# Block-quantizer scale computed straight from the block maximum, and layernorm statistics of the next tile taken before the transposes of this one

## What is computed

```python
def fp4_quant_dequant(x):                    # blocks of 16 along the last dim
    scale = jnp.max(jnp.abs(xb), axis=-1, keepdims=True) / 6.0
    scale = jnp.maximum(scale, jnp.float32(1e-12))
    xn = xb / scale
    idx = jnp.searchsorted(_MID, jnp.abs(xn))
    q = _GRID[idx] * jnp.sign(xn) * scale

mod = (_silu(c) @ wmod).reshape(B, 6, 1, -1)   # sa, ca, ga, sb, cb, gb
h = _layernorm(x) * (1 + ca) + sa
x = x + ga * attention(h, wq, wk, wv, wo)      # causal softmax, rope
h = _layernorm(x) * (1 + cb) + sb
gate, y = fp4_linear(h, w_gate), fp4_linear(h, w_up)
x = x + gb * fp4_linear(silu(gate) * y, w_down)
```

## Time and profile before

| what | value |
|---|---|
| time, median of 2 runs | 11339.54 us (11335.91 to 11343.18) |
| the profiled execution, its own time | 11276.26 us |
| its span, slowest core (core 4) | 11274.7 us |
| spans of the 8 cores | 11165.9 to 11274.7 us |
| VectorE busy on core 4 | 6960.9 us (62%) |
| TensorE matmul busy on core 4 | 5694.6 us (51%) |
| ScalarE busy on core 4 | 1098.6 us (10%) |

### The profile page before, as it was taken

One profiled execution on the slowest core, in us unless ns is written; L12 is line 12 of the kernel. 1 busy time (PEld: TensorE's weight loads), 2 busy tenths in 40 slices (PEclk: granted clock), 3 DMA queues, 4 the chain that ended last, 5 costly groups with the idle time before them and its releaser, 6 DMA issues.

```text
span 11274.7 us, 79773 instructions; the slowest of 8 cores (11165.9 to 11274.7 us)
## 1 busy us (share of the span) xinstructions
PE 5694.6 (51%) x20690; PEld 2189.5 (19%) x21080; DVE 6960.9 (62%) x17486; ACT 1098.6 (10%) x2066; POOL 100.6 (1%) x120
## 2 busy tenths in 40 slices
PE   1000156766675577467845454444554444544455
PEld 0000022212221222122212222222222222212222
DVE  6787753335324532443257777777777777777777
ACT  0000000220122013102300000000000000000000
POOL 0000000000000000000000000000000000000000
PEclk5555567766676788687867677767776777777777
DMA  3101121011101200211020000000000000000000
GB/s 66 49 30 55 50 32 30 30 36 25 30 30 43 25 23 30 52 15 38 15 82 15 12 12 13 14 12 12 15 10 14 12 14 13 10 14 12 15 12 12
DMA packets 181185, 289.77 MB, mean 26 GB/s; under 512 B 106428, under 2 KB 118972, under 8 KB 179720
## 3 DMA queue, kind: packets, MB, share of 16 engines
q1 hardware_dynamic: 63688, 237.28, 6.1%
q0 software_dynamic: 117056, 47.36, 3.6%
HBM read 247.45 MB, written 84.51 MB: 29 GB/s over the span
## 4 chain that ended last, share of the span: by engine, by line
DVE 43%; PE 28%; DVEq 13%; issue 7%; DMA 6%; ACT 2%; another core or an unknown queue 1%; POOL 1%; SPq 0%; ACTq 0%; POOLq 0%
DVEq L91 12%; PE pG L959 3%; PE pG L753 3%; PE pG L628 2%; DMA xt<-xmid_scr 2%; PE pA L607 2%; PE pA L705 2%; PE pB L607 2%; PE pEF L735 2%; PE pG L735 2%; DVE qd_g_f L443 2%; PE pC L730 2%; PE pH L939 2%; DVE qd_q_f L443 2%; PE pD L730 2%
## 5 line engine op out<-in xcount | busy, mean ns | idle before, releaser
L886 PE MATMUL pA<-wgT,xqf 128*128 128x512 bf16 x1461 | 633.7, 434 | 1157.7 <-DVE hmid L918 983.6
L959 PE MATMUL pG<-wdT,hqf 128*128 128x512 bf16 x2740 | 1006.7, 542 | 193.8 <-DVE hqf L944 186.5
L939 PE MATMUL pH<-identb,hq_t 128*128 128x128 bf16 x1408 | 180.6, 306 | 1288.5 <-DVEq L926 1288.5
L675 DVE COPY recipb<-pG 128x512 f32<-128x512 f32 x128 | 88.5, 692 | 1057.2 <-PE pG L669 1057.2
L892 PE MATMUL pC<-wuT,xqf 128*128 128x512 bf16 x1536 | 663.0, 432 | 44.2 <-DVE xqf L866 39.7
L726 ACT ACTIVATE union<-pA 128x512 bf16<-128x512 f32 (+1 forms) x640 | 354.7, 554 | 2759.3 <-PE pA L711 1717.3
L892 PE MATMUL pD<-wuT,xqf 128*128 128x512 bf16 (+1 forms) x1536 | 592.3, 386 | 6.0 <-issue 3.5
L886 PE MATMUL pB<-wgT,xqf 128*128 128x512 bf16 (+1 forms) x1473 | 570.3, 387 | 0.0
L959 PEld LDWEIGHTS pG<-wdT,hqf 128*128 128x128 bf16 x2816 | 352.5, 130 | 798.6 <-issue 732.2
L607 PE MATMUL pA<-union,wbuf 128*128 128x512 bf16 x1004 | 320.4, 473 | 260.7 <-DVE stag L613 103.0
L753 PE MATMUL pG<-union 128*128 128x512 bf16 x1000 | 340.9, 512 | 203.5 <-DVE xw L768 166.8
(11 more groups left out here) (163 smaller groups left out, 10556.1 us busy)
## 6 DMA issues: line engine op xcount, KB each, us to landing
xt<-x SPq DMA_DIRECT2D x128, 512.0 KB, 4.1
xmid_scr<-xw SPq DMA_DIRECT2D x64, 512.0 KB, 2.9
xt<-xmid_scr SPq DMA_DIRECT2D x64, 512.0 KB, 4.2
out<-xw SPq DMA_DIRECT2D x64, 512.0 KB, 2.8
wmb<-wmod POOLq DMA_DIRECT2D x12, 1024.0 KB, 10.4
wbuf<-wq POOLq DMA_DIRECT2D x32, 256.0 KB, 7.6
wbuf<-wk POOLq DMA_DIRECT2D x32, 256.0 KB, 6.9
wbuf<-wv POOLq DMA_DIRECT2D x32, 256.0 KB, 7.2
```

The source lines that it names most:

```text
L886: self.op('T', lambda E, cc=c, o=io, w=iw, p=pGt: E.matmul(p[:, 0:w], self.xqf[:, cc, :], self.wgT[:, cc, o:o + w], start=(cc == 0), stop= ...
L939: self.op('T', lambda E, cc=c, k2=kk, hq=hqt[i]: E.transpose(pH[:, k2, :], hq[:, cc * 128:(cc + 1) * 128], self.identb[:]), chT if kk == n ...
L959: st=(ib == 0 and c == 0), sp=lastd: E.matmul(pG[:, ha * 512:(ha + 1) * 512], self.hqf[:, k2, :], self.wdT[:, ig, ha * 512:(ha + 1) * 512] ...
```

## The change

Two edits that don't depend on each other.

In `_emit_qd` the intermediate `sc` is gone. The reciprocal is taken of `bm` itself, `scb` is computed from `bm` as `max(bm/6, 1e-12)`, and the factor 12 goes into the first constant of L423's instruction. One `tensor_scalar` for each piece and one fence for each call are removed. `scb`'s instruction now has two operations on its way (multiply, maximum), as the removed one had.

In stage A1 the load, the wait for it and the statistics of tile tc+1 are put between the layernorm of tile tc and the transposes and copy of tile tc. `_emit_ln_mod` is split into its two halves for this. TensorE's wait for `chV` stays the statement after them.

```diff
@@ _emit_qd
         each(lambda srcp, dstp, pw, nbl, src3, rs_b, sc_b, s:
-             V('V', lambda E: E.tensor_scalar(s['sc'][:, 0:nbl], s['bm'][:, 0:nbl],
-                                              1.0 / 12.0, 5e-13, ALU.mult, ALU.max)))
-        dr('V')
+             V('V', lambda E: E.reciprocal(s['rs'][:, 0:nbl], s['bm'][:, 0:nbl])))
         each(lambda srcp, dstp, pw, nbl, src3, rs_b, sc_b, s:
-             V('V', lambda E: E.reciprocal(s['rs'][:, 0:nbl], s['sc'][:, 0:nbl])))
-        each(lambda srcp, dstp, pw, nbl, src3, rs_b, sc_b, s:
-             V('V', lambda E: E.tensor_scalar(s['scb'][:, 0:nbl], s['sc'][:, 0:nbl],
-                                              2.0, None, ALU.mult)))
+             V('V', lambda E: E.tensor_scalar(s['scb'][:, 0:nbl], s['bm'][:, 0:nbl],
+                                              1.0 / 6.0, 1e-12, ALU.mult, ALU.max)))
         dr('V')
         each(lambda srcp, dstp, pw, nbl, src3, rs_b, sc_b, s:
              V('V', lambda E: E.scalar_tensor_tensor(
-                 s['xn'][:, 0:pw].rearrange("p (a b) -> p a b", b=16), src3, 1.0,
+                 s['xn'][:, 0:pw].rearrange("p (a b) -> p a b", b=16), src3, 12.0,
                  rs_b, ALU.mult, ALU.mult)))
@@ _emit_attention, stage A1
-        for tc in range(NTC):
+        def a1_stats(tc):
             b = tc % 2
             self.waitm('Y', self.r_xt.guard())
             self.dma('Y', self.xt[b][:], self.x_in[s, tc * 128:(tc + 1) * 128, :], dX[b])
             self.wait('V', dX[b])
-            self._emit_ln_mod(self.xt[b][:], self.hmod_t[:])
+            return self._emit_ln_stats(self.xt[b][:])
+
+        smark = a1_stats(0)
+        for tc in range(NTC):
+            b = tc % 2
+            self._emit_ln_apply(self.xt[b][:], self.hmod_t[:], smark)
             self.r_xt.done(chV)
+            if tc + 1 < NTC:
+                smark = a1_stats(tc + 1)
             self.wait('T', chV)
             self.waitm('T', self.r_pH.guard())
             for c in range(8):
```

## The result

| | before | changed |
|---|---|---|
| median | 11311.9 us (39 runs) | 11223.08 us (40 runs) |
| lowest | 11199.28 us | 11109.4 us |
| ratio | | 0.993, 95% interval 0.9907 to 0.9953 |
| span of the profiled execution, slowest core | 11274.7 us | 11161.4 us |
| VectorE busy, slowest core | 6960.9 us, 17486 instructions | 6874.2 us, 16838 instructions |

The account below looks back on a forecast made before the run. VectorE's ring of work and hand-overs was taken to bound the kernel. Quantizer -110.7 us, A1 move 0 and load 0 sum to -110.7 us: 11339.5 - 110, said as 11230 us, ratio 0.990, range 11165 to 11285 us.

Parts of the forecast that it names:

- what VectorE saves anywhere in the quantizer moves everything after it forward: Weight preparation and FFN: time saved in VectorE's quantizer shortens the path in full, 110.7 us.
- And no wait grows: FFN: VectorE's waits for down projection, load, transposes and `rstd` stay unchanged when the quantizer gets shorter.
- one ring: FFN: each VectorE wait begins when VectorE has delivered the awaited work's input; 358 of 1500 us idle is not slack.
- The price of the step: Quantizer: the removed step costs 0.345 us in 252 calls and 0.33 us in 72 short ones, 110.7 us.
- The second operation: Quantizer, `scb`'s instruction: a second operation on its way is free, taken as 0 us.
- The bound of 23 us: Quantizer: at worst `scb`'s new pair costs L413's 0.27 us instead of 0.20, 324 x 0.07 us.
- The gap of the fence: Quantizer: the removed step's 0.08 us of fence goes too; the reciprocals move up to where L413 stood.
- rival 2: Quantizer gives back less, 64 to 88 us instead of 111, through fence gap or `scb`'s pair: 11252 to 11275 us; chance 0.16.
- The A1 move: Stage A1: TensorE's wait also counts the next tile's statistics, so -6 to +6 us over 60 tiles, taken as 0.
- Rival 1: Stage A1: the move does hide the hand-over, up to 83 us more gain, 11147 us; chance 0.04.
- The load: Stage A1: loads get 6.8 us from issue to reader against a median landing of 3.5; no wait within a sequence.
- rival 5: Whole run: an offset, the same program took 11276 and 11343 us; at the lower, about 11166 us; chance 0.07.

Follow-up runs that it names:

- e6_ffn_order: Changed kernel with the FFN's up-projection product of block k put ahead of the copy of block k-1's transposes; ratio 0.9755 to the kernel before, FFN 5256.3 us.
- e7_xt3: Changed kernel with a third xt buffer in the FFN and each load issued one tile earlier; ratio 0.9698 to the kernel before, FFN 5201.1 us.
- e5_fence: Changed kernel with one more fence per quantizer call, between reciprocals and bfloat16 scale; one execution, weight preparation grows by 16.4 us, FFN by 70.8 us.
- e2_a1_only: Kernel before with the A1 edit alone; ratio 0.9985 (0.9937 to 1.0033).
- e3_a1_mark: Changed kernel with TensorE's A1 wait given the count right after the layernorm; ratio 0.9851 to the kernel before, A1 tile 5.22 us.
- e1_quant_only: Kernel before with the quantizer edit alone; ratio 0.9939 (0.9892 to 0.9987).
- e4_step_twice: Kernel before with the removed small scale step and its fence done twice; ratio 1.0111 (1.003 to 1.0191).

## Why the prediction was right

**The bound.** The step "what VectorE saves anywhere in the quantizer moves everything after it forward" held in the stages: 110.0 us against 110.7 in the sum. "And no wait grows" did not hold in full: the wait for the last down projection grew by 8 us, though the FFN stage shows no such loss. That the waits are one ring, `e6_ffn_order` and `e7_xt3` show by other pieces of it. (The heading of the earlier trace rows names rows 3; the call beside it is that of the earlier trace rows.)

**The price of the step.** 0.345 and 0.33 us for 324 calls gave 23.3 us for weight preparation and 87.4 for the FFN. Measured are 23.4 and 86.6, alone 23.1 and 88.3, and added a second time 25.1 and 88.3. Busy time fell by 86.7 us, 87 were forecast.

**The second operation.** Taken as 0, from L443 against L448; L415's mean is 139 ns, as was that of L419 in the kernel before. The bound of 23 us rested on L413's 178 ns. `e5_fence` shows where that came from: behind a fence both instructions of the very same pair take 178 ns in the mean (L416 in that run), so it is its place and neither its type nor its operations. The prediction had named place and type and left it open.

**The gap of the fence.** It did not stay ahead of the reciprocal (0.07 us stand there, as stood ahead of L413 before); rival 2 did not come.

**The A1 move.** "-0.1 to +0.1 us on each tile, I take 0": it was +0.05 us, 3 us in all, and `e2_a1_only` shows 0.9985 (0.9937 to 1.0033). That the count in TensorE's wait is the cause, and not the move itself, is shown by `e3_a1_mark`. Rival 1 would have been worth 60 x (6.64 - 5.22) = 85 us against the kernel before, where 83 were written.

**The load.** No wait within a sequence, as forecast. The cover of 6.8 us was 6.8, the landing as VectorE sees it 3.5 to 4.

**The whole time.** 11230 us were forecast and 11223.08 measured, but that this is so close owes something to chance: the kernel before had a median of 11311.9 in those runs, not 11339.54, and the difference of the medians is 89 us, not 110. The forecast ratio of 0.990 lies just outside the interval of 0.9907 to 0.9953. In the stages that the change touches nothing is missing, so the rest lies outside them, most likely in attention, whose slowest core differs from profile to profile by more than that. The low clock of some cores does not explain all of it: over all cores on record with a granted clock of 0.71 or more, the median span is 11187.5 us before (124 cores) and 11088.4 changed (137 cores), 99 us less, and `e1_quant_only` (39 cores) and `e4_step_twice` (12 cores) stand 101 below and 103 above the kernel before, where their stages make 111 and 113. So some 10 us of the price of the step do not reach the whole time, and where they go is open. What the prediction lacked is a sentence on this spread: it read the 0.6% between two executions as an offset of a run (rival 5), and in the profile of before the slowest core's excess stands in attention (4380.4 us, median 4289.9).

**A misreading without effect.** "5 us for the next tile's load" was the mean over 59 waits that held the first tiles of the sequences; a usual one is 4.3 us.

## What to carry to other kernels

A move that lets an engine work during a hand-over is only as good as the count that the other engine waits for: when work that raises a shared semaphore is put in front of a wait for "everything so far", the wait moves with it, so give the wait the value of its real producer. In a chain of small dependent VectorE steps, price a step from start to start (here 0.34 us for 0.27 us of instructions), multiply by the calls, and check that every wait on the ring begins with a delivery of the same engine; then the product is the gain. Where the slowest of 8 cores is measured and one stage spreads, read the effect in the stages.

## What the runs showed of the hardware

- An explicit fence between two VectorE lines that don't depend on each other costs 0.22 us here by its timeline and 0.24 to 0.28 us by the stages, not the 0.08 us of gap that stands at the fence: the lines lose their overlap of 0.08 us, and each of the two small instructions behind it takes 178 ns in the mean, where 139 is the mean without the fence.
- A `tensor_scalar` with a multiply and a maximum takes the same time as one with a multiply alone: 139 ns at 128x32 for both (L419 before, L415 after).
- Two cores of one execution can differ by 171 us in attention (granted clock 0.77 against 0.71) (`e1_quant_only`, cores 0 and 2). In the FFN, where VectorE's ring sets the pace, granted clocks of 0.72 and of 0.66 to 0.67 on the two halves of the chip go with 5434.2 and 5440.1 us, 0.1% apart (changed kernel).
